# Graph attention on one core: a different order of work on TensorE and VectorE within a slot

## The reference, cut to what matters

```python
h = relu(layernorm(x))                        # per node, over 384 features
q, k, v = h @ Wq + bq, h @ Wk + bk, h @ Wv + bv   # six heads of 64
scores = einsum('bhqd,bhkd->bhqk', q, k) / sqrt(64)
probs = softmax(scores + where(adj, 0.0, -9e15), axis=-1)
ctx = einsum('bhqk,bhkd->bhqd', probs, v)     # heads side by side: 384 again
out = x + ctx @ Wf + bf
```

## Time and profile before

| what | us |
|---|---|
| median of three runs (955.02 to 957.18) | 955.31 |
| the profiled execution, its own time | 957.55 |
| span of the profiled execution, first to last instruction | 955.7 |
| PE busy in it | 914.5 |
| DVE busy | 818.6 |
| ACT busy | 764.2 |
| POOL busy | 592.4 |

### The profile page before, as it was taken

The page is one execution under the profiler, slowest core; times in us unless marked ns, Lnnn a source line. Parts: engine busy times, 40 slices in busy tenths (PEclk is TensorE's granted clock), DMA queues, the critical chain, the costliest instruction groups (busy, mean ns, idle before and its releaser), DMA issues.

```text
span 955.7 us, 25344 instructions
## 1 busy us (share of the span) xinstructions
PE 914.5 (96%) x8649; PEld 525.5 (55%) x8649; DVE 818.6 (86%) x1301; ACT 764.2 (80%) x2245; POOL 592.4 (62%) x587
## 2 busy tenths in 40 slices
PE   3989999999999999999999999999999999999966
PEld 1445555555555555555555555555555555555533
DVE  6688889988988988998898899889889889987863
ACT  4587888888888888888888888888888888887662
POOL 4466666666666666666666666666666666654341
PEclk9999999999999999999999999999999999999987
DMA  8458787767777776776777677677677767856653
GB/s 239 106 132 152 170 160 176 181 156 171 176 173 167 178 173 153 173 184 161 171 173 174 164 176 181 149 179 177 165 169 173 182 154 175 183 129 134 128 120 96
DMA packets 374175, 156.08 MB, mean 163 GB/s; under 512 B 323329, under 2 KB 374145, under 8 KB 374145
## 3 DMA queue, kind: packets, MB, share of 16 engines
q1 hardware_dynamic: 374144, 155.70, 71.1%
HBM read 54.99 MB, written 25.17 MB: 84 GB/s over the span
## 4 chain that ended last, share of the span: by engine, by line
PE 91%; DVE 4%; ACT 2%; issue 1%; DMA 1%; POOL 1%; SPq 0%; DVEq 0%; POOLq 0%
PE ps_m L268 39%; PE ps_qk L268 38%; PE ps_m L376 7%; PE ps_s L352 7%; DMA w_raw_f<-in_L_gnn_Wf 1%; ACT s L446 1%; DVE s L620 1%; DVE neg_max L629 1%; DVE parts L666 1%; DVE ct_lo L658 0%; DVE y L592 0%; ACT k_hi L428 0%; POOL h_parts L774 0%; ACT ct_hi L457 0%; POOL shift L747 0%
## 5 line engine op out<-in xcount | busy, mean ns | idle before, releaser
L446 ACT ACTIVATE s<-s,neg_max 128x128 f32<-128x128 f32 x768 | 296.5, 390 | 3.9 <-DVE neg_max L629 3.9
L793 POOL TENSOR_TENSOR s<-s,inv_sums 128x768 f32<-128x768 f32 x128 | 189.4, 1480 | 176.2 <-DVE inv_sums L612 176.2
L268 PE MATMUL ps_m<-w_hi_v,ht 128*128 128x384 f16 x768 | 208.2, 326 | 0.0
L784 POOL TENSOR_TENSOR x_res<-x_res,out_bias 128x768 f32<-128x768 f32 x64 | 116.9, 1826 | 132.6 <-DMA x_res<-in_x 132.6
L268 PE MATMUL ps_qk<-ht,w_hi_q 128*128 128x512 f16 x576 | 173.5, 383 | 1.0 <-DVE q_lo L603 1.0
L268 PE MATMUL ps_qk<-ht,w_hi_k 128*128 128x512 f16 x576 | 171.3, 379 | 2.2 <-DVE q_lo L603 2.2
L666 DVE TENSOR_TENSOR parts<-s,parts 128x768 f16<-128x768 f32 x128 | 142.0, 1109 | 11.2 <-ACT parts L466 11.2
L446 ACT ACTIVATION_READ_ACCUMULATOR s<-s,neg_max 128x1 f32 x768 | 146.5, 191 | 0.0
L457 ACT ACTIVATE ct_hi<-ps_m 128x768 f16<-128x768 f32 x64 | 51.9, 811 | 117.7 <-PE ps_m L376 117.7
L268 PE MATMUL ps_m<-w_hi_f,ct_hi 128*128 128x384 f16 x384 | 128.3, 334 | 11.1 <-DVE ct_lo L658 11.1
L620 DVE SCALAR_TENSOR_TENSOR s<-ps_s,unscale,mask 128x768 f32<-128x768 f32 x128 | 129.6, 1012 | 4.6
(11 more groups left out here) (77 smaller groups left out, 1732.8 us busy)
## 6 DMA issues: line engine op xcount, KB each, us to landing
x_in<-in_x SPq DMA_DIRECT2D x64, 384.0 KB, 3.2
x_res<-in_x SPq DMA_DIRECT2D x64, 384.0 KB, 3.5
out<-y SPq DMA_DIRECT2D x128, 192.0 KB, 2.3
adj_in<-in_adj SPq DMA_DIRECT2D x32, 64.0 KB, 2.8
pt<-parts SPq DMA_TRANSPOSE x128, 4.4
ht<-h_parts SPq DMA_TRANSPOSE x64, 3.8
w_raw_q<-in_L_gnn_Wq SPq DMA_DIRECT2D x1, 576.0 KB, 4.2
w_raw_k<-in_L_gnn_Wk SPq DMA_DIRECT2D x1, 576.0 KB, 7.2
```

Source lines behind the costliest of these rows:

```text
L268: last = mm(psum, parts_a[a](i), parts_b[b](i), start=n == 0, stop=n == len(todo) - 1)
L446: last = activation(s[:, i, hd, :], s[:, i, hd, :], ACT.Exp, bias=neg_max[:, i, hd:hd + 1], accum_out=sums[:, i, hd:hd + 1])
L784: nc.gpsimd.tensor_tensor(x_res[:, r, :, :], x_res[:, r, :, :], out_bias[:, :].unsqueeze(1).to_broadcast([128, 2, FEAT]), ALU.add).then_in ...
L793: nc.gpsimd.tensor_tensor(s[:, i, :, :], s[:, i, :, :], inv_sums[:, i, :].unsqueeze(2).to_broadcast([128, HEADS, NODES]), ALU.mult).then_i ...
```

## The change

PE's slot has `projection(0)` between the first and the second q/k tile in place of behind the second. DVE's slot begins with `lower_context` in place of the masked scores; `residual(0)` comes ahead of `spread`; and `qk_lower(1)` comes ahead of `mean_and_variance`. No instruction is added or removed, and ACT, POOL and SP have the same programs.

```diff
@@ PE, slot
                 qk_tile(0)
+                projection(0)
                 qk_tile(1)
-                projection(0)
                 values(0)
                 qk_tile(2)
                 values(1)
@@ DVE, slot
+                lower_context()
                 masked_scores(1, t - 1)
-                lower_context()
                 maxima(1, t - 1)
                 qk_lower(0)
                 reciprocals(0)
+                residual(0)
                 spread()
                 spread_done()
-                residual(0)
+                qk_lower(1)
                 mean_and_variance()
-                qk_lower(1)
                 reciprocals(1)
                 lower_v(0)
                 lower_probs(0)
```

## The result

| | before | changed |
|---|---|---|
| median of 15 runs each, us | 955.6 (953.92 to 959.29) | 959.84 (957.61 to 962.2) |
| the profiled execution, us | 957.55 | 962.18 |
| its span, us | 955.7 | 960.4 |

The ratio of the changed kernel to the one before is 1.0036, 95% interval 1.0025 to 1.0047: some 3.4 us slower (955.6 x 0.0036); the two medians are 4.2 apart, inside that interval.

What follows compares the result with a forecast made beforehand. PE was taken to bound the kernel, its columns running without gaps in the loop. PE's new waits, 2.5 + 0.5 = 3.0 us, with nothing for DVE, were added to the 955.31 median: 958.3 us, range 955.2 to 962.2.

Steps and rivals of the forecast that it cites:

- What bounds the kernel: In the loop, 90 to 904 us, PE waits for nobody; its pace is that of its columns, 14.02 us a slot.
- the chain against the first tile: Ahead of `projection(0)`: `ct_hi`, `ct_lo` and their hand-overs take 1.965 or 2.05 us, against 1.96 (1.955) of q/k matmuls.
- two kinds of slots: In the loop, `ct_hi` starts 0.105 or 0.19 us after the first q/k matmul, half each; slots of 14.03 and 14.12.
- +3.0 us: PE's waits ahead of `projection(0)` over 58 slots: 2.5 us in the long kind plus 0.5 in the short.
- `ct_lo` itself: DVE's `ct_lo`, between `ct_hi` and PE's `projection(0)`, was put at 0.95 us.
- The hand-overs: `ct_hi` to `ct_lo` 0.03 us, `ct_lo` to `projection(0)`'s first matmul 0.06, and 0.01 more to the second.
- the weight load: The load ahead of `projection(0)` can't run early but costs little; a page estimate would charge 0.107 us a slot, 6.2 in all.
- DVE's reserve: DVE stands 0.54 us ahead of `lower_context`, about 0.4 left after the new order; no cost taken for DVE's part.
- the list of signs: What the changed trace should show, among it DVE idle about 0.5 us ahead of `ct_lo`.
- ACT's idle time ahead of `ct_hi`: With `k_hi` 0.5 us later behind the second q/k tile, ACT's idle there should fall from 1.75 us.
- the rival: In the loop, the new small gaps bring PE's clock down: 104 us more, 1059; chance 0.02.
- the 0.3% border: Whole kernel: 0.3%, 2.9 us, is what a measurement can tell from no change; border 958.2; chance of slower 0.50.

Runs made afterwards that it cites:

- the second experiment: The changed kernel with DVE's masked scores put back ahead of `lower_context`, PE's order as changed: 985.47 us, ratio 1.0292 to the kernel before.
- the fourth experiment: The changed kernel with the first of the second q/k tile's nine matmuls moved ahead of `projection(0)`: 957.53 us, ratio 1.0006 to the kernel before.
- the first experiment: The changed kernel with `projection(0)` back behind the second q/k tile, DVE's order as changed: 956.95 us, ratio 0.9993 to the kernel before.

## Why the prediction was right, and where it was off

- **What bounds the kernel.** Right: PE's columns in the loop, without a gap before. The kernels in which the projection found `ct_lo` ready all had slots of 14.02, whatever DVE's order (but for the loop's fourth slot, above).
- **The mechanism.** Right in place and kind: the chain against the first tile, in two kinds of slots. They were put at 14.03 and 14.12 us and came at 14.04 to 14.05 and 14.13. Putting one matmul of cover back took the whole loss away.
- **The size, +3.0 us against 3.4 by the ratio and 3.6 in the trace's loop.** The mis-sized term is `ct_lo` itself. I took 0.95 from the earlier trace rows, where it followed another instruction of DVE without a break. In the new order DVE stands idle ahead of it, and then it takes 0.96: in the slots above, and at the end of the kernel before. Where DVE came to it without a break, as in the second experiment, it is 0.95. 57 x 0.01 = 0.6 us, and 3.0 + 0.6 = 3.6. The medians over the loop bear it out: 947 ns before, 958 in the changed kernel, 948 in the second experiment's. It is as much as the prediction had allowed for the rows' resolution, so that the sum came this near is in part luck. The earlier trace rows was the row for the state that the change makes, and I had used it for the hand-overs only.
- **The hand-overs and the weight load.** Right: 0.03, 0.05 to 0.06 and 0.01 as in the earlier trace rows. The second projection matmul comes 0.17 behind the first; the Trainium skill's page "TensorE: Matmul & The Clock Gate" (LDWEIGHTS) gives 107 ns for a load of 128 columns, and the trace agrees on the load's length: the one at 473.55 is listed with 0.10. But the estimate that an exposed load costs PE that much doesn't hold here: its matmul starts at 473.56.
- **DVE's reserve.** Right: DVE stands 0.38 to 0.46 us ahead of `ct_lo` in the slots shown, 24.5 us over 58 slots or 0.42 each, where the working had 0.4 (and the list of signs 0.5). With PE's old order the move of the lower part cost nothing (ratio 1.0001).
- **ACT.** Half wrong, at no price: `k_hi` does wait for PE now, 26.2 us over 59 slots or 0.44 each, and starts 5.67 us behind the slot's first q/k matmul in place of 5.13. But ACT's idle time ahead of `ct_hi` is 1.75 as it was the earlier trace rows, not less. In the timeline of ACT in the changed kernel these are the rows of `k_hi` and of the slot's last work ahead of the next `ct_hi`, in the slot from 485.63:

```profile
491.30 0.69 ACT L428 ACTIVATE k_hi<-ps_qk,qk_bias 128x512 f16<-128x512 f32 x1 [0.44 <-PE ps_qk L268]
...
497.37 0.84 ACT L487 ACTIVATE h_parts<-h 128x768 f16<-128x768 f32 x1
```

  In the kernel before, in the slot from 469.19, the last one is

```profile
480.81 0.84 ACT L487 ACTIVATE h_parts<-h 128x768 f16<-128x768 f32 x1
```

  That is 11.62 us into the slot before and 11.74 now. Of 0.54 us all but 0.12 was made up within the slot, and the slot of 14.13 us, 0.11 longer, gave back the rest; in which gaps, the list of waits doesn't show.
- **The clock.** Right: 1.00 in the loop with 58 new gaps, so the rival didn't come about. The Trainium skill, in "TensorE: Matmul & The Clock Gate" (A second HAM failure mode: psum-queue depth-cycling), tells of a clock that swings on frequent short idles; no run here shows it. The gaps of these runs are 0.01 to 0.5 us (the second experiment's kernel too ran the loop without a fall); longer ones no run here shows in the loop.
- **Slower or not.** The sum lay on the 0.3% border, and so does the result: 0.36%, with an interval of 0.25 to 0.47 that has the border in it. On which side of it the single figure came out is no merit of the working.

## What to carry to other kernels

Where the bounding engine has no gaps, moving one of its operations forward doesn't shorten its own stretch, and it may make it wait: add up the chain that releases it from its event, subtract the work that stands ahead of it on the engine, and take durations from rows in the state that the new order makes (idle ahead or not). A few hundredths of a microsecond per slot appear neither in the engine's busy row nor in its list of waits; measure from start to start over many slots, and look at the weight loads' waits. An engine whose busy row has no gap can still be held by its sequencer: a wait that ends later, ahead of a loop's branch, cost 0.07 us or more here. Of two waits ahead of one operation, see which stands on the operation itself. A partial cover is cheap to try: one matmul of 0.22 us moved across the wait gave the whole loss back.

## What the runs showed of the hardware

- An execution's time goes with its mean granted clock. Of the changed kernel's own runs, spans were 955.8 us at a mean clock of 0.995, 958.4 at 0.991 and 960.0 to 960.4 at 0.987. All of the profiled loops ran at 1.00. The gap of 3.2 us ahead of the loop is in each trace, yet from 74 to 90 us the clock was 0.89 and 0.84 in the two kernels compared and 1.00 in the profile of the fourth experiment, whose span is 952.3:

```profile
74.00:90.00 16.00, 16.00 (x176) 9.49 (x172) 14.16 (x22) 12.55 (x37) 11.62 (x11) 1.00 0.93 175
```

  So one profiled span is no measure of a change of 3 us here, and the fall behind that gap doesn't come each time. What decides it wasn't tried.
- ACT's `ct_hi` with two semaphores to wait for started 0.19 us behind the first q/k matmul in half of the loop's slots, those in which the wait that ends last stood on a register instruction ahead of it; with one wait, 0.11 or less in all.
- DVE's `ct_lo` (128 x 768) took 0.96 us where DVE had stood idle ahead of it, and 0.94 to 0.95 where it followed another operation without a break.
- From the loop's branch on PE's sequencer to the first matmul behind it passed 0.58 to 0.64 us in the slots of the first experiment in which PE stood for it.
